# Written-out step lists for four engines, and sorted rows stored from ScalarE's queue

## The reference

```python
x = x + L0_xattn(ctx, norm(x))  # (1-g)*h + g*(A+A^T)/2, A = sigmoid(sim) where sim is in its row's top 76, sim = QK^T of ctx
x = x + L0_ffn(norm(x))         # MXFP8 quantise-dequantise by blocks of 32; silu(gate) * up, quantised again; down
x = x + L1_xattn(norm(x), ctx)  # 16 heads: project, rope, softmax(scores), context, output projection
x = x + L1_ffn(norm(x))         # router picks 1 of 32 experts per token: x @ (ternary weight * that expert's mask) * scale * prob
```

## Time and profile before

| | before |
|---|---|
| three runs | 654.73, 655.03, 656.84 us (median 655.03) |
| the profiled execution | 652.0 us |
| its span, first to last instruction | 650.2 us |
| PE busy, 3221 matmuls | 501.6 us (77%) |
| VectorE / ScalarE / GpSimd busy | 373.8 / 233.2 / 261.1 us |
| mean granted TensorE clock | 0.92 of full |

### The profile page before, as it was taken

The page is one execution under the profiler, slowest core; times in us unless marked ns, Lnnn a source line. Parts: engine busy times, 40 slices in busy tenths (PEclk is TensorE's granted clock), DMA queues, the critical chain, the costliest instruction groups (busy, mean ns, idle before and its releaser), DMA issues.

```text
span 650.2 us, 9473 instructions
## 1 busy us (share of the span) xinstructions
PE 501.6 (77%) x3221; PEld 330.9 (51%) x3221; DVE 373.8 (57%) x737; ACT 233.2 (36%) x626; POOL 261.1 (40%) x268
## 2 busy tenths in 40 slices
PE   2872686767798579879998697889977989756696
PEld 1752335445554447545556474555555756534442
DVE  2999884479666713986565349766641452300254
ACT  1752221143432312436334133453432256333243
POOL 2766244259737732422123423231224321215066
PEclk9985898898997879989999799899997999966799
DMA  7950100023314220012220100121201002226000
GB/s 281 367 204 0 66 0 5 1 81 122 122 41 121 81 62 0 1 30 61 79 70 33 32 1 2 45 59 57 70 17 33 0 22 62 58 73 178 16 2 17
DMA packets 38256, 41.83 MB, mean 64 GB/s; under 512 B 7168, under 2 KB 33408, under 8 KB 37312
## 3 DMA queue, kind: packets, MB, share of 16 engines
q1 hardware_dynamic: 37920, 40.43, 19.4%
q0 software_dynamic: 288, 0.79, 0.4%
HBM read 34.13 MB, written 7.08 MB: 63 GB/s over the span
## 4 chain that ended last, share of the span: by engine, by line
PE 48%; DVE 25%; issue 9%; ACT 9%; POOL 8%; DMA 1%; SPq 0%; POOLq 0%; DVEq 0%; ACTq 0%
PE qc L598 10%; PE ga L598 10%; PE s L598 8%; PE qb L598 6%; PE ua L598 5%; PE tp L601 4%; PE tp L598 3%; DVE simwk L1228 3%; DVE top L1226 2%; POOL moe L1645 2%; ACT reg L995 2%; ACT moe L917 2%; DVE amax L1153 2%; DVE reg L1300 2%; DVE small L1200 1%
## 5 line engine op out<-in xcount | busy, mean ns | idle before, releaser
L1585 POOL TENSOR_TENSOR reg<-reg,rsum 128x512 f32<-128x512 f32 x64 | 69.0, 1099 | 175.8 <-DVE rsum L1314 175.8
L917 ACT COPY reg<-tp 128x512 f32<-128x512 f32 (+1 forms) x100 | 51.3, 513 | 104.9 <-PE tp L601 95.7
L995 ACT ACTIVATE reg<-s,nmax 128x256 f32<-128x256 f32 x128 | 59.0, 476 | 54.2 <-DVE nmax L1307 54.1
L601 PE MATMUL tp<-idn,reg 128*128 128x128 f32 x296 | 51.6, 299 | 32.6 <-ACT reg L953 21.6
L598 PE MATMUL qc<-reg,wM 128*64 128x256 f32 (+1 forms) x384 | 68.6, 402 | 7.4 <-DVE et L1395 5.0
L598 PE MATMUL qb<-reg,wA_hi 128*128 128x256 f16 x384 | 69.2, 287 | 2.7 <-ACT reg L980 2.7
L1307 DVE TENSOR_REDUCE nmax<-s 128x2 f32<-128x512 f32 x64 | 40.9, 680 | 41.3 <-PE s L598 41.3
L601 PEld LDWEIGHTS tp<-idn,reg 128*128 128x128 f32 x296 | 34.5, 149 | 52.8 <-ACT reg L953 24.0
L1300 DVE TENSOR_TENSOR reg<-qb,cosq 128x768 f32<-128x768 f32 x32 | 30.5, 955 | 53.5 <-PE qb L598 53.2
L598 PEld LDWEIGHTS qc<-reg,wM 128*64 128x64 f32 (+1 forms) x384 | 38.5, 159 | 27.6 <-issue 17.8
L598 PE MATMUL s<-reg 64*128 64x256 f32 x256 | 38.2, 417 | 14.3 <-issue 12.8
(11 more groups left out here) (210 smaller groups left out, 968.5 us busy)
## 6 DMA issues: line engine op xcount, KB each, us to landing
masks<-in_moe_masks SPq DMA_DIRECT2D x16, 512.0 KB, 3.7
wtile<-wE_d SPq DMA_DIRECT2D x120, 64.0 KB, 1.7
y_d<-masks SPq DMA_DIRECT2D x15, 256.0 KB, 2.3
wM<-in_att_wq SPq DMA_DIRECT2D x1, 2048.0 KB, 8.4
wtile<-in_wo_t SPq DMA_DIRECT2D x1, 2048.0 KB, 12.7
wE_d<-moe SPq DMA_DIRECT2D x16, 128.0 KB, 1.9
reg<-in_kc_q SPq DMA_DIRECT2D x1, 1536.0 KB, 11.6
reg<-in_qr_t SPq DMA_DIRECT2D x1, 1536.0 KB, 19.6
```

The costliest lines, as they stand in the source:

```text
L601: return nc.tensor.transpose(dst, src, idn[:, :])
L917: nc.scalar.copy(dst, src).then_inc(bank.drained, 1)
L995: nc.scalar.activation(attn[p % 2][:, k * S:(k + 1) * S], s.tensor[:, (k % 2) * S:(k % 2 + 1) * S], ACT.Exp, bias=nmax[:, o:o + 1], accum_ ...
L1585: nc.gpsimd.tensor_tensor(a, a, rsum[:, o + 2 * hh:o + 2 * hh + 2].unsqueeze(2).to_broadcast([P, 2, S]), ALU.mult).then_inc(attn_ready.sem, 1)
```

## The change

The tables and `tensor_order` go. Each engine gets flat lists: a setup, three loop bodies (iteration 0; 1 and 2; 3; a step's first number is its batch relative to b), and a tail, played by `steps_of`. The steps are finer: a projection's three tiles, each half of `row_max`, `softmax` and `attention`, three parts of a quantisation, 19 single rounds of the search, gate and value of an FFN step, each half of `hidden_turn`, and `pick` (the one-hot matrix) apart from `rank`. The order is new on every engine. `ffn_down` of the second half, the third quantisation and the last `row_max` and `row_sum` of a batch lie in the next loop body; group order on PE is 0, 2, 1, 4, 3 in iterations 1 and 2; in iterations 1 and 2 GpSimd's `unsort` comes before its last `attention`; `expert_weights` begins at once in iteration 0. The stores of sorted rows go from SP to ScalarE's queue, one behind each `group`. Matmuls, tiles and sizes are the same. What the prediction speaks of, cut from a diff of 1,423 lines:

```diff
 
...
     for b in range(B):
-        more = b + 1 < B
-        moe = moe_beside(b)
-        steps += [("keys_turn", b), ("x_turn", b)]
...
-    6: ([('ffn_up', 1)], []),
-    7: ([], []),
-}]
-
-NORM_STEP = [3, 3]
...
+TENSOR_LOOP = [
...
+    [
+        ("attn_turn", -1, 6, 1), ("ffn_down", 0, 1), ("context", -1, 6), ("keys_turn", 0), ("adj_qk", 1),
+        ("x_turn", 0), ("adj_sim", 1), ("project", 0, 0, 0), ("attn_turn", -1, 7, 0), ("project", 0, 0, 1),
+        ("project", 0, 0, 2), ("attn_turn", -1, 7, 1), ("context", -1, 7), ("to_keys", 0, 0), ("project", 0, 1, 0),
+        ("project", 0, 1, 1), ("scores", 0, 0), ("project", 0, 1, 2), ("att_out", -1), ("project", 0, 2, 0),
+        ("project", 0, 2, 1), ("to_keys", 0, 1), ("project", 0, 2, 2), ("scores", 0, 1), ("moe_turn", -1),
+        ("logits", -1), ("project", 0, 3, 0), ("project", 0, 3, 1), ("project", 0, 3, 2), ("to_keys", 0, 2),
+        ("attn_turn", 0, 0, 0), ("scores", 0, 2), ("attn_turn", 0, 0, 1), ("rank", -1), ("project", 0, 4, 0),
+        ("context", 0, 0), ("tiles", -1), ("project", 0, 4, 1), ("attn_turn", 0, 1, 0), ("project", 0, 4, 2),
+        ("to_keys", 0, 3), ("attn_turn", 0, 1, 1), ("gather", -1, 0), ("context", 0, 1), ("gather", -1, 1),
+        ("gather", -1, 2), ("adjacency_turn", 1), ("attn_turn", 0, 2, 0), ("scores", 0, 3), ("project", 0, 5, 0),
+        ("attn_turn", 0, 2, 1), ("project", 0, 5, 1), ("to_keys", 0, 4), ("project", 0, 5, 2), ("gather", -1, 3),
+        ("context", 0, 2), ("gather", -1, 4), ("project", 0, 6, 0), ("attn_turn", 0, 3, 0), ("to_keys", 0, 5),
+        ("gather", -1, 5), ("project", 0, 6, 1), ("attn_turn", 0, 3, 1), ("scores", 0, 4), ("project", 0, 6, 2),
+        ("ffn_in", 1), ("context", 0, 3), ("ffn_gate", 1, 0), ("ffn_value", 1, 0), ("ffn_gate", 1, 1),
+        ("group", -1, 0), ("ffn_value", 1, 1), ("project", 0, 7, 0), ("ffn_gate", 1, 2), ("scores", 0, 5),
+        ("attn_turn", 0, 4, 0), ("to_keys", 0, 6), ("group", -1, 2), ("ffn_value", 1, 2), ("group", -1, 1),
+        ("attn_turn", 0, 4, 1), ("project", 0, 7, 1), ("scores", 0, 6), ("project", 0, 7, 2), ("context", 0, 4),
+        ("ffn_gate", 1, 3), ("attn_turn", 0, 5, 0), ("ffn_value", 1, 3), ("attn_turn", 0, 5, 1), ("to_keys", 0, 7),
+        ("hidden_turn", 1, 0, 0), ("hidden_turn", 1, 0, 1), ("group", -1, 4), ("group", -1, 3), ("context", 0, 5),
+        ("ffn_down", 1, 0), ("attn_turn", 0, 6, 0), ("hidden_turn", 1, 1, 1), ("hidden_turn", 1, 1, 0),
+        ("scores", 0, 7),
+    ],
...
+        ("group", -1, 0), ("project", 0, 7, 0), ("scores", 0, 5), ("project", 0, 7, 1), ("attn_turn", 0, 4, 0),
+        ("attn_turn", 0, 4, 1), ("to_keys", 0, 6), ("group", -1, 1), ("context", 0, 4), ("group", -1, 2),
+        ("project", 0, 7, 2), ("attn_turn", 0, 5, 0), ("scores", 0, 6), ("attn_turn", 0, 5, 1), ("to_keys", 0, 7),
+        ("group", -1, 3), ("context", 0, 5), ("group", -1, 4), ("attn_turn", 0, 6, 0), ("scores", 0, 7),
+    ],
...
+SCALAR_SETUP = [
+    ("gam_tanh",), ("adj_qk", 0), ("adj_tanh", 0), ("adj_norm", 0), ("fold_q", 0), ("fold_q", 1), ("fold_q", 2),
+    ("fold_q", 3), ("fold_q", 4), ("fold_q", 5), ("fold_q", 6), ("fold_q", 7), ("fold_k", 0), ("ffn_norm", 0),
+    ("fold_k", 1), ("fold_k", 2), ("turn_w", 0, 0), ("turn_w", 0, 1), ("fold_k", 3), ("fold_k", 5), ("turn_w", 0, 3),
+    ("turn_w", 0, 2), ("turn_w", 1, 1), ("fold_o", 0), ("turn_w", 1, 3), ("turn_w", 1, 0), ("turn_w", 1, 2),
...
+SCALAR_LOOP = [
...
+    [
+        ("keys_turn", 0), ("x_norm", 0), ("adj_qk", 1), ("x_turn", 0), ("attn_turn", -1, 7, 0),
+        ("attn_turn", -1, 7, 1), ("adj_tanh", 1), ("context", -1, 7), ("to_keys", 0, 0), ("softmax", 0, 0, 0),
+        ("softmax", 0, 0, 1), ("to_keys", 0, 1), ("moe_norm", -1), ("moe_turn", -1), ("softmax", 0, 1, 0),
+        ("softmax", 0, 1, 1), ("to_keys", 0, 2), ("route_exp", -1), ("attn_turn", 0, 0, 0), ("attn_turn", 0, 0, 1),
+        ("softmax", 0, 2, 0), ("context", 0, 0), ("softmax", 0, 2, 1), ("attn_turn", 0, 1, 0), ("to_keys", 0, 3),
+        ("attn_turn", 0, 1, 1), ("gather", -1, 0), ("context", 0, 1), ("gather", -1, 1), ("gather", -1, 2),
+        ("adj_norm", 1), ("attn_turn", 0, 2, 0), ("attn_turn", 0, 2, 1), ("softmax", 0, 3, 0), ("softmax", 0, 3, 1),
+        ("gather", -1, 3), ("ffn_norm", 1), ("context", 0, 2), ("to_keys", 0, 4), ("gather", -1, 4),
+        ("attn_turn", 0, 3, 0), ("gather", -1, 5), ("attn_turn", 0, 3, 1), ("ffn_in", 1), ("softmax", 0, 4, 0),
+        ("ffn_up", 1, 0), ("context", 0, 3), ("softmax", 0, 4, 1), ("ffn_up", 1, 1), ("group", -1, 0),
+        ("store", -1, 0), ("to_keys", 0, 5), ("ffn_up", 1, 2), ("softmax", 0, 5, 0), ("to_keys", 0, 6),
+        ("softmax", 0, 5, 1), ("attn_turn", 0, 4, 0), ("group", -1, 2), ("store", -1, 2), ("group", -1, 1),
+        ("attn_turn", 0, 4, 1), ("context", 0, 4), ("store", -1, 1), ("softmax", 0, 6, 0), ("ffn_up", 1, 3),
+        ("attn_turn", 0, 5, 0), ("softmax", 0, 6, 1), ("hidden_turn", 1, 0, 0), ("attn_turn", 0, 5, 1),
+        ("to_keys", 0, 7), ("group", -1, 4), ("group", -1, 3), ("hidden_turn", 1, 0, 1), ("store", -1, 4),
+        ("context", 0, 5), ("store", -1, 3), ("attn_turn", 0, 6, 0), ("hidden_turn", 1, 1, 1),
+        ("hidden_turn", 1, 1, 0), ("softmax", 0, 7, 0), ("softmax", 0, 7, 1), ("attn_turn", 0, 6, 1),
+        ("context", 0, 6),
+    ],
...
+        ("softmax", 0, 4, 1), ("to_keys", 0, 5), ("group", -1, 0), ("context", 0, 3), ("softmax", 0, 5, 0),
+        ("attn_turn", 0, 4, 0), ("attn_turn", 0, 4, 1), ("softmax", 0, 5, 1), ("store", -1, 0), ("context", 0, 4),
+        ("group", -1, 2), ("to_keys", 0, 6), ("group", -1, 1), ("attn_turn", 0, 5, 0), ("store", -1, 1),
+        ("store", -1, 2), ("softmax", 0, 6, 0), ("softmax", 0, 6, 1), ("to_keys", 0, 7), ("attn_turn", 0, 5, 1),
+        ("group", -1, 3), ("context", 0, 5), ("group", -1, 4), ("attn_turn", 0, 6, 0), ("store", -1, 3),
+        ("store", -1, 4),
+    ],
...
+VECTOR_SETUP = [
+    ("adj_sim", 0), ("top", 0, 0), ("top", 0, 1), ("gam_scales",), ("top", 0, 2), ("top", 0, 3), ("adj_stats", 0),
+    ("top", 0, 4), ("top", 0, 5), ("top", 0, 6), ("top", 0, 7), ("top", 0, 8), ("top", 0, 9), ("top", 0, 10),
+    ("top", 0, 11), ("quant_w", 0, 0), ("top", 0, 12), ("top", 0, 13), ("top", 0, 14), ("top", 0, 15),
+    ("top", 0, 16), ("quant_w", 0, 1), ("top", 0, 17), ("top", 0, 18), ("quant_w", 0, 2), ("masked", 0),
+    ("adjacency_out", 0), ("quant_w", 1, 0), ("quant_w", 1, 1), ("quant", 0, 0, 0), ("quant_w", 1, 2),
+    ("quant", 0, 0, 1), ("quant", 0, 0, 2), ("quant_w", 2, 0), ("quant_w", 2, 1), ("quant_w", 2, 2),
+    ("ffn_up", 0, 0), ("ffn_up", 0, 1), ("quant", 0, 1, 0), ("quant", 0, 1, 1), ("ffn_up", 0, 2), ("quant", 0, 1, 2),
+    ("ffn_up", 0, 3), ("quant", 0, 2, 0), ("quant", 0, 2, 1), ("quant", 0, 2, 2), ("ffn_down", 0, 0), ("ternary",),
...
+VECTOR_LOOP = [
...
+    [
+        ("quant", 0, 2, 0), ("quant", 0, 2, 1), ("quant", 0, 2, 2), ("ffn_down", 0, 0), ("row_max", -1, 7, 0),
+        ("row_max", -1, 7, 1), ("row_sum", -1, 7), ("ffn_down", 0, 1), ("x_turn", 0), ("adj_sim", 1), ("top", 1, 0),
+        ("rotate", 0, 0), ("top", 1, 1), ("top", 1, 2), ("top", 1, 3), ("top", 1, 4), ("top", 1, 5), ("top", 1, 6),
+        ("row_max", 0, 0, 0), ("adj_stats", 1), ("top", 1, 7), ("top", 1, 8), ("row_max", 0, 0, 1),
+        ("row_sum", 0, 0), ("rotate", 0, 1), ("att_out", -1), ("top", 1, 9), ("top", 1, 10), ("top", 1, 11),
+        ("rotate", 0, 2), ("row_max", 0, 1, 0), ("row_max", 0, 1, 1), ("route", -1), ("row_sum", 0, 1),
+        ("top", 1, 12), ("top", 1, 13), ("rotate", 0, 3), ("row_max", 0, 2, 0), ("rank", -1), ("top", 1, 14),
+        ("row_max", 0, 2, 1), ("tiles", -1), ("top", 1, 15), ("pick", -1), ("row_sum", 0, 2), ("top", 1, 16),
+        ("top", 1, 17), ("top", 1, 18), ("masked", 1), ("route_sum", -1), ("rotate", 0, 4), ("adjacency_out", 1),
+        ("row_max", 0, 3, 0), ("row_max", 0, 3, 1), ("row_sum", 0, 3), ("rotate", 0, 5), ("quant", 1, 0, 0),
+        ("quant", 1, 0, 1), ("quant", 1, 0, 2), ("row_max", 0, 4, 0), ("row_max", 0, 4, 1), ("ffn_up", 1, 0),
+        ("row_sum", 0, 4), ("rotate", 0, 6), ("ffn_up", 1, 1), ("quant", 1, 1, 0), ("row_max", 0, 5, 0),
+        ("row_max", 0, 5, 1), ("quant", 1, 1, 1), ("row_sum", 0, 5), ("quant", 1, 1, 2), ("ffn_up", 1, 2),
+        ("row_max", 0, 6, 0), ("rotate", 0, 7), ("row_max", 0, 6, 1), ("ffn_up", 1, 3), ("row_sum", 0, 6),
+    ],
...
+POOL_SETUP = [
+    ("zero",), ("th1", 0), ("rstd", 0, 0), ("fold_low", 0), ("fold_low", 1), ("fold_low", 2), ("fold_low", 3),
+    ("fold_low", 4), ("fold_low", 5), ("fold_low", 6), ("fold_low", 7), ("zero_shared",), ("dequant_w", 0),
+    ("rstd", 0, 1), ("ffn_in", 0), ("dequant_w", 1), ("dequant_w", 2), ("ffn_up", 0, 0), ("ffn_up", 0, 1),
+    ("keys", 0), ("rstd", 0, 2),
+]
+
+POOL_LOOP = [
+    [
+        ("expert_weights", 1, 0), ("expert_weights", 1, 1), ("expert_weights", 1, 2), ("rstd", 1, 0),
```

(50 more changed lines are left out.)

832 lines of the change are left out of this document (350 added, 482 removed), and 5 rows, old and new, of tables (FILLS, POOL_TAIL).

## The result

The changed kernel takes **582.16 us**, the median of 4 runs (581.07 to 582.20), beside 654.88 us (651.46 to 656.84) for the kernel before in runs on the same chip: a ratio of 0.889 with a 95% interval of 0.885 to 0.893. The profiled execution took 582.17 us with a span of 580.4. Some executions of a kernel run over 1.5% longer than its fastest, at a lower clock; two of the ten of e12 are such, and its median leaves them out.

What follows compares the result with a forecast made beforehand. PE was taken to bound iterations 1 and 2, so its idle time and lower clock could be won. Terms 0 - 13 - 10 - 10 - 13 + 0 = -46 from 652.0, plus 3.0 to the median, gave 609.0 us; range 591 to 634.

Steps and rivals of the forecast that it cites:

- Setup, forecast 0: Setup: the collision of VectorE and GpSimd over their shared port could stay, go or come twice; 0, between -4 and +4.
- Iteration 3, forecast -13: Iteration 3: stores on ScalarE's queue remove PE's 11.1 us gap, loads bind by at most 2 us; between -9 and -17.
- Iterations 1 and 2, forecast -10 each: Iterations 1 and 2: boundary, ranking, clock and finer steps gain, store issues cost +1; -10 each, between -4 and -14.
- The ranking's 6.07: Ranking: PE's three waits shrink by 4 of 6.07 us as `pick` and a `rotate` leave VectorE's path and PE has other work.
- The boundary's waits: Before `x_turn` in iterations 1 and 2: PE gets filler work, 4.17 us falls to about 1.5; -3, and -1.5 for the clock.
- The +1 for five stores on ScalarE: Iterations 1 and 2: issuing five stores costs ScalarE at most 5.5 us, mostly in its idle time; +1.
- Iteration 0, forecast -13: Iteration 0: GpSimd's early expert weights and the boundary cut PE's waits; -4, -3, -3 and -3, between -6 and -20.
- The term for the waits for `attention`: Iteration 0: early expert weights take away most of PE's 4.43 us wait for `attention` and two similar, shorter ones.
- The 5.55 us: Iteration 0, PE's wait in front of a `hidden_turn`: goes in half, as two pairs of expert weights remain on GpSimd there.
- the rival that it holds ScalarE: Slower: each store's issue holds ScalarE 4.1 us with PE waiting, 15 stores cost 61 us, 670 us; chance 0.04.
- The stores were not late because of SP: Rival: the transfer, or loads and stores hindering each other, made the wait; the 11.1 us stay, 620 us; chance 0.07.
- every gap finds its filler: Rival: iterations 1 and 2 reach 107 us, iteration 0 102, iteration 3 79; 585 us in all; chance 0.12.

Runs made afterwards that it cites:

- e12: Kernel before with three parts together: stores from ScalarE's queue, GpSimd's new order in iteration 0, the filled boundary; 642.15 us, ratio 0.982.
- e2: Changed kernel with only the stores put back on SyncE, behind the 40 loads of their batch; 603.59 us.
- e11: Changed kernel with batch 2's inputs loaded earlier and `keys_turn` ahead of `x_turn` at the last boundary; 575.36 us, ratio to before 0.880.
- e1: Kernel before with only the five stores of sorted rows per batch issued from ScalarE's queue; 648.06 us, ratio 0.991.
- e7: Changed kernel with `pick` put back directly behind `rank` on VectorE; 583.04 us.
- e3: Changed kernel with only GpSimd's list of iteration 0 put back to the old order; 604.94 us.
- e5: Kernel before with only GpSimd's steps of iteration 0 in the new order, expert weights ahead of attention; 648.12 us, ratio 0.991.
- e9: Kernel before with only the boundary between iterations filled, `adj_qk` ahead of `x_turn` and `context` behind the last `ffn_down`; 652.50 us, ratio 0.998.

## Why the prediction was wrong

The sign was right, and the size was not. What failed are three terms of the sum, each of which came out beyond its own lower bound: iteration 0 with -24.7 us for -13 (bound -20), and iterations 1 and 2 with -15.5 and -16.8 for -10 (bound -14). They make up 24.0 us of the miss of 27; 3.0 more is the step from the profiled execution to the median, which is nothing in the changed kernel (582.17 and 582.16). The other three terms together were off by 0.3. By its own steps:

**Setup, forecast 0, came +0.9.** Right, and by the mechanism named: the collision moved. `masked` took 5.13 us (2.86 before) and ended 0.3 us after GpSimd's 4.63 us subtraction, and `adjacency_out` took 2.04 instead of 4.58, so the two nearly cancel. The same setup took 116.2 to 118.9 us in the kernels of e2 to e11 that have it, so +0.9 itself says little. The exclusive lock of the Trainium skill (SBUF — State Buffer, section "SBUF: two separate sides") agrees with both traces. **End, forecast 0, came -1.8**: inside its bounds, busy time down by 0.5 and the clock 0.89 for 0.86.

**Iteration 3, forecast -13, came -11.8.** Right for the changed kernel: idle time fell by 11.0 us, and the loads hold up nothing there. The +1.6 for a copy that waits for store 0 didn't come. But the 11.1 us aren't the stores' alone. e1 shows that moving the stores alone gives 5.9, since SyncE's 40 loads bind then. In the new order the copies begin while the loads still go out, and TensorE's work ahead of the last group fills the 45.36 us.

**Iterations 1 and 2, forecast -10 each, came -15.5 and -16.8.** In iteration 1, idle time fell by 14.3 us. The ranking's 6.07 all went, where I took 4, and not for the reason I gave first (e7). The boundary's waits (4.17, 0.68 and 0.67) became 1.31, -4.2 against -3. The rest, waits under 1 us each, gave 4.0 where I had counted 1.5 of some 7. The +1 for five stores on ScalarE didn't come: 0.37 us each, and nobody waits. Busy time fell by 1.2, where I had 2.5 for the clock, which the stretch's mean clock doesn't show. So the terms for idle time were sized at 7.5 us net and measured 14.3: I kept a remainder in each, and the remainders had one sign. In iteration 2 idle time fell by 13.3 us and busy time by 3.5, of which some 1.6 is work that moved to its neighbours.

**Iteration 0, forecast -13, came -24.7**, the largest miss: idle time fell by 21.0 us and busy time by 3.7, at the higher clock. The term for the waits for `attention`, 7.8 us in three, was sized well: -7, and 1.1 is left. The boundary gave some 2.3 for 3, as the context is late. The 5.55 us went whole and not in half, though "two pairs of expert weights (5.7 us) remain on GpSimd there". And the sum put at nothing, without a reason, two waits of TensorE for VectorE and one of 1.75 us for ScalarE, which all went. The first two, in the kernel before:

```profile
158.64 0.66 PE L601 MATMUL ga<-idn,simwk 128*128 128x128 f32 x4 [3.60 <-DVE simwk L1236]
...
198.96 2.08 PE L598 MATMUL ga<-wGU,ffn 128*128 128x512 f32 x2 [3.23 <-DVE sg L1263]
```

The changed kernel has no wait over 0.9 us between 126 and 212 us. e3 shows that GpSimd's list carries 23 us of this in the new order, with all the idle time back, and e5 that it carries 5.9 in the old. I had added up TensorE's waits one by one. With GpSimd's list and TensorE's made for each other nearly all went at once, those that name another engine too. That GpSimd alone was the cause in the old kernel is not shown; its list alone brings 5.9 there.

**Stores.** ScalarE's issue was rightly put under 1.1 us; the rival that it holds ScalarE is refuted. "The stores were not late because of SP" is refuted by e2.

**The rivals.** What happened is "every gap finds its filler": forecast 107, 107, 102 and 79 us for iterations 1, 2, 0 and 3, measured 110.3, 109.4, 97.3 and 83.8. I gave it 0.12 and left it out of the range. The reason I gave for the middle case was that each gap would keep a remainder; the profile held a sign against that which I read and didn't use: in iterations 1 and 2 no engine but TensorE passes 78 of 126 us, and TensorE's longest single wait is 4.17 us. With lists free to be reordered on all engines, these two came out 2.7 and 1.4 us above TensorE's old busy time; a sum over named waits with a remainder in each was the pessimistic case.

**What the experiments say of the cause.** Undone one at a time in the new kernel, the stores, GpSimd's list, the boundary and the fine steps cost 21.4, 22.8, 18.0 and 23.9 us, 86 in sum and more than the whole gain of 72.7. Done one at a time in the old kernel, the first three bring 5.9, 5.9 and 1.2, and 11.6 together. So the prices are not shares of the gain: each is what one old part costs in lists that were made for the new one. My reading of the rows is that a part that is missing opens gaps, with a drop of the clock behind them, and a part that is added alone moves its gap to the next thing that is late. Not shown: how TensorE's order in the middle of the iterations shares in it by itself, since no kernel had only that order; and that ScalarE's and VectorE's lists are needed too is inferred from the remainder of e12, not measured apart.

## What to carry to other kernels

When a change reorders all in-order engines together, bound it by the busiest engine's busy time in each stretch, and give that case a real chance; the sum over named waits is the price of single edits, and these e1, e5 and e9 show to be small. Price a wait on TensorE with what the clock may lose behind it: here taking away a wait of 2.60 us, with 1.32 left in its place, was worth 4.1 to 5.4 us. And before work is moved to fill a gap, look at what it covered where it stood.

## What was unexpected of the hardware

A store costs an engine's queue little: 0.37 us from ScalarE, 0.38 for the stores of expert weights from SyncE. The 40 tile loads, whose address is read from a table into a register each time, take 1.13 us each (45.36 / 40), three times as much. The queue was slow because of these, not because of the stores' transfers (a store lands in 2.3 us from either engine). That the register read is what costs the time is not measured apart.

TensorE's granted clock made a good part of several results: 0.62 behind a boundary with waits of 2.72, 4.16 and 0.68 us, against 0.82 behind one with 1.31. But a wait has no fixed price. In e9 the same sixteen matmuls stand twice behind a wait of 2.63 us, and take 3.69 us at the end of iteration 1 and 5.38 at the end of iteration 2. A wait of 0.77 us in a busy stretch shows no loss: the eight matmuls of `context` behind one, at 430.58 us of the changed kernel, take 1.09 us, as in the earlier trace rows.
